# Attention stage of a decoder layer: weight columns laid out for contiguous stack reads, one DMA for the aug rows, a semaphore for each row part

## The chip, the cores and the metric

The kernel runs on one core of one Trainium2 chip. The metric is the device time of one execution in microseconds. Three runs of the kernel before took 932.71, 935.84 and 937.98 us; the median is 935.84.

## The reference

The program is one post-norm decoder layer on x (4 batches of 512 tokens, 256 features) with a context of the same shape:

```
x = layernorm(x + attn(x))                 # one head of 256, causal softmax
x = layernorm(x + xattn(q=x, k=ctx, v=ctx))
x = layernorm(x + ffn(x))                  # 8 experts, the best 2 for each token, and a shared expert

def xattn(q, k, v):                        # 16 heads of 16 features, blocks of 128 tokens
    Q, K, V = (heads(t @ W.T + b) for ...)
    loc   = softmax(Qb @ Kb.T / 4) @ Vb                      # the query's own block
    cross = softmax(Qb @ K[window of 3 blocks].T / 4) @ V    # own block and its neighbours
    return (loc + cross) @ Wo.T + bo
```

Everything is in float32. The kernel gets that accuracy on TensorE by splitting operands into a high and a low part (float32r) and summing high x high, high x low and low x high.

## The kernel before

**Stages.** The attention stage treats the batches one after the other and takes the first 450 us. Then come routing and the shared expert, then 39 tiles of 128 slots for the experts, then the last norm. The change is in the cross attention alone.

**Halves.** The 16 heads of a batch are treated in two halves of 8. `half(a, c)` on PE (L1466) has 16 units. In each it computes, for half `a`, raw scores of two heads (L1507), from which VectorE takes maxima (L1023), and for the half `c` before it the scores again, now with the maxima subtracted (L1522 for the own block, L1528 for the neighbours), which ScalarE exponentiates (L697) and PE multiplies with V (L1473, L1487). So half `a` and half `c` run interleaved, one stage apart. Between two halves PE has other work: the first attention of the next batch (`glue_and_attention1`) or the projections of the next batch (`project2`).

**The stack.** A head has only 16 features. To fill TensorE's rows, the three products of high and low parts are stacked: `k_stack` holds for each pair of heads 32 partitions of high rows, 32 of low and 32 of high again; `q_stack` holds for each head its high, high and low rows, at partitions 32 * section + 16 * parity, the other 16 partitions of a section being zero. So one matmul of 96 rows gives the full product. Rows 96 to 99 of `q_stack` are the aug rows: the negated maxima and their differences, in high and low parts, which meet ones in `k_stack`.

**How a stack is filled.** The projections leave keys and queries with features on partitions. SP writes them to DRAM, high and low separately (`rows_away`, L263, into `k_rows` and `q_rows`), waits for those writes, and reads them back into the stack (`stack`): 3 DMAs of 256 KB for the keys (L275) and 12 of 64 KB for the queries (L283). The feature order is head by head, so the 512 tokens of one feature, 2 KB, are what lies together on the DRAM side when heads of one half are read into one partition. PE waits for the keys and the first six query reads before a half (`stacked`, L1501) and for the other six at its middle (`stacked_late`, L1503). The aug rows go from `augT` (32 partitions) to four partitions of `q_stack` by four DMAs, one for each (`aug_rows`, L290).

**What sets the order.** SP issues all these DMAs, in program order, in one queue; a wait of SP holds up all that is behind it. From one batch to the next the order is: key rows of half 0, aug rows of half 1 of the batch before, query rows of half 0, loop edge, keys and queries of the stack of half 0, key and query rows of half 1, x_raw; later aug rows of half 0, the stack of half 1, c_raw. `keep_clock` is a run of matmuls without use that only occupies PE.

Of the kernel before, what the change touches and what calls it, by code (L numbers as in the profile page):

```python
# [21 lines left out]
F = mybir.dt.float32  # L22
# [3 lines left out]
ALU = mybir.AluOpType  # L26
AX = mybir.AxisListType.X

P = 128
B, S, D = 4, 512, 256  # L30
# [5 lines left out]
HEADS, DH = 16, 16  # L36
HALF = HEADS // 2
# [23 lines left out]
PAIRS = HALF // 2  # L61
# [8 lines left out]
def build(nc, x_d, xT_d, cT_d, w_d, brow_d, bcol_d, gate_w_d, gate_b_d,  # L70
          w1_d, b1T_d, w2_d, b2_d, ws1_d, bs1T_d, ws2_d, bs2_d, out_d):
    ctx = ExitStack()
    with ctx:  # L73
# [3 lines left out]
        def sem(name):  # L77
            return ctx.enter_context(nc.semaphore(name))
# [143 lines left out]
                                            for n in ("xs_in", "yw_sent", "st_step", "st_sent"))  # L222
        k_away, q_away, stacked, stacked_late = ([sem(f"s_{n}{h}") for h in range(2)]
                                                 for n in ("k_away", "q_away", "stacked", "stacked_late"))
# [13 lines left out]
        def _(sp):  # L238
# [20 lines left out]
            def rows_away(b, h, rows, src, away, j):  # L259

                for part, ready in enumerate(("qk2_hi", "qk2_lo")):
                    sp.wait_ge(s[ready], 4 * b + 2 * h + j)
                    sp.dma_start(rows[h, part], src[:, h, part, :].bitcast(F)).then_inc(away[h], 16)  # L263

            def keys_away(b, h):
                rows_away(b, h, k_rows, k_s, k_away, 1)

            def queries_away(b, h):
                rows_away(b, h, q_rows, q_s, q_away, 2)

            def stack(b, h):

                sp.wait_ge(k_away[h], 32 * b + 32)
                for sec, part in ((0, 0), (2, 0), (1, 1)):
                    sp.dma_start(k_stack[32 * sec:32 * sec + 32, h * PAIRS:(h + 1) * PAIRS, :].bitcast(F),  # L275
                                 k_rows[h, part].rearrange("(g p) t -> p g t", g=PAIRS)).then_inc(stacked[h], 16)
                sp.wait_ge(q_away[h], 32 * b + 32)
                for part_done, g0 in ((stacked, 0), (stacked_late, PAIRS // 2)):
                    for par in range(2):
                        for sec, part in enumerate((0, 0, 1)):  # L280
                            r = 32 * sec + 16 * par
                            at = h * HALF + 2 * g0 + par
                            sp.dma_start(q_stack[r:r + 16, at:at + HALF // 2 - 1:2, :].bitcast(F),  # L283
                                         q_rows[h, part].rearrange("(g a p) t -> a p g t", g=PAIRS, a=2)
                                         [par][:, g0:g0 + PAIRS // 2, :]).then_inc(part_done[h], 16)

            def aug_rows(b, h):
                sp.wait_ge(s["augT_out"], 2 * b + h + 1)
                for r in range(4):
                    sp.dma_start(q_stack[96 + r:97 + r, h * HALF:(h + 1) * HALF, :].bitcast(F),  # L290
                                 augT[r * HALF:(r + 1) * HALF, :].bitcast(F)).then_inc(s["aug_in"], 16)

            def body(b, first, last):
# [5 lines left out]
                stack(b, 0)  # L299
                keys_away(b, 1)  # L300
                queries_away(b, 1)
# [13 lines left out]
                stack(b, 1)  # L315
                if not last:
                    sp.wait_ge(s["v_set"], b + 1)
                    sp.dma_start(c_raw[:, :, :], cT_d[:, bass.ts(nb, S)].rearrange("(k p) t -> p k t", p=P))\
                        .then_inc(s["c_raw_in"], 16)
                    keys_away(b + 1, 0)  # L320
                aug_rows(b, 1)
                if not last:
                    queries_away(b + 1, 0)

            keys_away(0, 0)
            queries_away(0, 0)
# [261 lines left out]
        def _(act):  # L588
# [6 lines left out]
            def aug_rows(a, free):  # L595
                if free:
                    act.wait_ge(s["aug_in"], 64 * a)
                act.wait_ge(s["augT_ps"], a + 1)
                copy(augT[:, :], ps[0:4 * HALF, 3, :], "augT_out")
# [55 lines left out]
            def project2(b, c, g):  # L655
# [9 lines left out]
                if c is not None:  # L665
                    for h in range(2):
                        act.wait_ge(k_away[h], 32 * b)
                        act.wait_ge(q_away[h], 32 * b)
# [170 lines left out]
        def _(dve):  # L839
# [175 lines left out]
            def half(a, c, h, ln=None):  # L1015

                if a is not None:
# [12 lines left out]
                    at = 3 * a  # L1030
                    dve.wait_ge(s["a_red"], UNITS * a + UNITS)
# [3 lines left out]
                    nc.vector.tensor_copy(aug[:, :, 0, :], ncross[:, :, :]).then_inc(s["aug_step"], 1)  # L1035
                    dve.wait_ge(s["aug_step"], at + 2)
                    nc.vector.tensor_tensor(aug[:, :, 1, :], ncross[:, :, :], aug[:, :, 0, :].bitcast(F), ALU.subtract)
                    nc.vector.tensor_copy(aug[:, :, 2, :], dloc[:, h, :, :]).then_inc(s["aug_step"], 1)
                    dve.wait_ge(s["aug_step"], at + 3)
                    nc.vector.tensor_tensor(aug[:, :, 3, :], dloc[:, h, :, :], aug[:, :, 2, :].bitcast(F), ALU.subtract)\  # L1040
# [246 lines left out]
        def _(pe):  # L1287
# [178 lines left out]
            def half(b, a, c, ha, hc, full, v2=None):  # L1466
# [26 lines left out]
                if c is not None:  # L1493
                    pe.wait_ge(s["k_ones"], 1)
                    pe.wait_ge(s["aug_in"], 64 * (c + 1))
                for u in range(UNITS):
                    if a is not None:
# [14 lines left out]
                    if c is not None:  # L1512
# [8 lines left out]
                        qv = q_stack[:, 2 * p:2 * p + 2, :]  # L1521
# [254 lines left out]
```

## Time and profile before

| | |
|---|---|
| median of 3 runs | 935.84 us |
| the profiled execution's own time | 933.65 us |
| its span | 931.9 us, mean granted clock 0.907 |
| PE busy | 830.1 us (89%) |
| VectorE, ScalarE, GpSimd busy | 397.5, 346.7, 242.0 us |
| DMA | 76.83 MB, mean 82 GB/s |
| PE at L1507 (raw scores) | 88.9 us, idle before it 16.2 us |

Busy time is the time in which an engine executes; "idle before" is the time for which it stood still ahead of a group of instructions, with what it waited for. PEclk (also "granted clock") is the TensorE clock that the throttle granted, as a share of 2.4 GHz. The profile shows one execution; its 933.65 us is 2.19 below the median of the three timed runs.

### The profile page before, as it was taken

What the parts mean: (1) busy time and instruction counts of PE and PEld (TensorE: products, weight loads), DVE (VectorE), ACT (ScalarE), POOL (GpSimd) and SP (SyncE); (2) the same over time, 40 slices, a digit from 0 to 9 for tenths busy, and PEclk for the clock granted to TensorE, in tenths of its full rate; (3) what the DMA queues carried; (4) which work ended last, traced back from release to release, by engine and by line L of the source; (5) the groups of instructions that cost most, each with busy time, mean ns of one, the idle gap of its engine ahead of it and who ended that gap; (6) DMA issues with size and microseconds to landing.
All of it is one profiled execution on the core that took longest, in us unless ns stands there. A gap on an engine that the chain in (4) does not pass through costs nothing. (4 is left out here: it accounts for less than half of the span.)

```text
span 931.9 us, 15553 instructions
## 1 busy us (share of the span) xinstructions
PE 830.1 (89%) x4992; PEld 626.3 (67%) x4993; DVE 397.5 (43%) x746; ACT 346.7 (37%) x898; POOL 242.0 (26%) x258
## 2 busy tenths in 40 slices
PE   6689988999898989999579998999999999999930
PEld 4567765777567656766479997666777777666620
DVE  4736574568346844452376552211222222222216
ACT  1122454346343633255254430333333333333313
POOL 6912111123111401020416775211111111111106
PEclk9987995799669975999889999999999999999975
DMA  9962133121404080300191115541111101111035
GB/s 305 159 178 51 47 94 91 44 52 50 135 2 91 19 231 3 70 4 2 49 363 42 57 52 131 182 158 34 34 34 34 33 29 34 34 34 32 19 108 179
DMA packets 61045, 76.83 MB, mean 82 GB/s; under 512 B 16112, under 2 KB 41584, under 8 KB 60880
## 3 DMA queue, kind: packets, MB, share of 16 engines
q1 hardware_dynamic: 57600, 66.99, 25.9%
q0 software_dynamic: 3408, 9.34, 2.8%
q8 instruction: 23, 0.38, 0.2%
q14 instruction: 14, 0.11, 0.0%
HBM read 50.82 MB, written 24.98 MB: 81 GB/s over the span
## 5 line engine op out<-in xcount | busy, mean ns | idle before, releaser
L1023 DVE TENSOR_REDUCE mx<-ps 128x4 f32<-128x512 f32 (+1 forms) x128 | 104.4, 821 | 95.4 <-PE ps L1507 93.9
L1694 PE MATMUL ps<-we,hT 128*128 x624 | 142.8, 382 | 2.5 <-ACT hT L795 2.5
L1694 PEld LDWEIGHTS ps<-we,hT 128*128 128x128 f32 x624 | 119.7, 192 | 35.5 <-issue 20.9
L1674 PE MATMUL ps<-we,xT 128*128 x312 | 140.6, 593 | 1.9 <-issue 1.9
L1224 DVE COPY hp<-ps 128x512 f32<-128x512 f32 x78 | 50.2, 686 | 158.5 <-PE ps L1674 158.5
L1507 PE MATMUL ps<-k_stack,q_stack 96*128 96x256 f32 (+1 forms) x256 | 88.9, 441 | 16.2 <-DMA q_stack<-q_rows 14.2
L795 ACT ACTIVATE hT<-ps,b1T 128x128 f32<-128x128 f32 x312 | 84.9, 383 | 35.2 <-PE ps L1685 35.2
L1674 PEld LDWEIGHTS ps<-we,xT 128*128 128x128 f32 x312 | 56.2, 190 | 58.1 <-issue 58.1
L697 ACT ACTIVATE pT<-ps 128x256 f32<-128x256 f32 x128 | 49.2, 385 | 117.9 <-PE ps L1522 113.1
L1507 PEld LDWEIGHTS ps<-k_stack,q_stack 96*128 96x128 f32 x256 | 50.6, 246 | 54.5 <-issue 24.4
L590 ACT ACTIVATE xT<-ps 128x256 f32<-128x256 f32 x39 | 14.9, 384 | 180.9 <-PE ps L1657 180.9
L566 POOL CAST yidx<-meta 128x1 int32 (+1 forms) x39 | 7.2, 184 | 238.6 <-ACT yw L804 238.6
L700 ACT ACTIVATE pT<-ps 128x256 f32<-128x256 f32 (+1 forms) x128 | 62.4, 487 | 0.9
L232 PE MATMUL ps<-xT_s,ws_s 128*128 128x256 f32 x384 | 49.8, 291 | 11.0 <-DVE xT_s L841 9.2
L1232 DVE TENSOR_TENSOR ysum<-ps,b2b 128x256 f32<-128x256 f32 x39 | 16.6, 424 | 95.2 <-PE ps L1694 95.2
L232 PEld LDWEIGHTS ps<-xT_s,ws_s 128*128 128x128 f32 x384 | 48.7, 200 | 11.7 <-issue 11.7
L1528 PE MATMUL ps<-q_stack,k_stack 98*128 98x256 f32 (+1 forms) x128 | 54.3, 424 | 0.0
L1292 PE MATMUL ps<-w_s 128*128 128x512 f32 x218 | 52.2, 393 | 0.0
L232 PE MATMUL ps<-ws_s,h_s 128*128 128x256 f32 x384 | 47.9, 284 | 0.0
L232 PEld LDWEIGHTS ps<-ws_s,h_s 128*128 128x128 f32 x384 | 46.5, 191 | 0.5 <-DVE ws L1144 0.5
L569 POOL DMA_INDIRECT pair_out<-yw,yidx x39 | 38.2, 980 | 29.6 <-POOL yidx L566 29.6
L1292 PEld LDWEIGHTS ps<-w_s 128*128 128x128 f32 x218 | 40.1, 188 | 8.1 <-issue 0.2
(214 smaller groups left out, 1246.1 us busy)
## 6 DMA issues: line engine op xcount, KB each, us to landing
we<-in_w SPq DMA_DIRECT2D x16, 1024.0 KB, 10.6
k_stack<-k_rows SPq DMA_DIRECT2D x24, 256.0 KB, 4.0
q_stack<-q_rows SPq DMA_DIRECT2D x96, 64.0 KB, 4.1
slot_rows<-attn SPq DMA_DIRECT2D x1, 4992.0 KB, 25.0
xs<-slot_rows SPq DMA_DIRECT2D x39, 128.0 KB, 2.1
k_rows<-k_s SPq DMA_DIRECT2D x16, 256.0 KB, 2.3
q_rows<-q_s SPq DMA_DIRECT2D x16, 256.0 KB, 2.8
yl<-pair_out SPq DMA_DIRECT2D x4, 1024.0 KB, 9.5
```

The costliest lines, as they stand in the source:

```text
L232: m = nc.tensor.matmul(out, lhs(a), rhs(b), start=first and n == 0, stop=last and n == 2, skip_group_check=check)
L569: pool.indirect_dma_start(out=pair_out, out_offset=bass.IndirectOffsetOnAxis(ap=yidx[:, q, :], axis=0), in_=yw[:, q, :], in_offset=None).t ...
L697: nc.scalar.activation(pT[:, m % 2, u % 2, 0:2 * P], ps[:, bank, 256:512], ACT.Exp, scale=SCALE2)\
L700: nc.scalar.activation(pT[:, m % 2, u % 2, 2 * P:2 * P + w], ps[:, bank + 1, 0:w], ACT.Exp, scale=SCALE2).then_inc(s["b_exp"], 1)
L795: last = nc.scalar.activation(hT[:, c, :], ps[:, 4 + c // 4, (c % 4) * P:(c % 4 + 1) * P], ACT.Gelu, bias=b1T[:, bass.ds(e * NH + c, 1)])
L1023: nc.vector.tensor_reduce(mx[:, n, 2 * p:2 * p + 2, r0:r0 + nb], ps[:, 2 * (u % 2):2 * (u % 2) + 2, 0:nb * P].rearrange("p h (b k) -> p h ...
L1224: last = nc.vector.tensor_copy(hp[:, c * 512:(c + 1) * 512], ps[:, 2 + c, :])
L1292: nc.tensor.matmul(ps[:, bank, :], w[:, 0:P], w, start=True, stop=True)
L1507: m = nc.tensor.matmul(ps[:, 2 * (u % 2) + j, 0:nb * P], q_stack[0:96, ha * HALF + 2 * p + j, n * P:(n + 1) * P], k_stack[0:96, ha * (HALF ...
L1528: nc.tensor.matmul(ps[:, bank + 1, 0:w].rearrange("p (h n q) -> p h n q", h=2, q=P), k_stack[0:98, p, i * P:(i + 1) * P], qv[0:98, :, :].r ...
L1674: m = nc.tensor.matmul(ps[:, 2 + c, :], xT[:, q, k, :], w[:, bass.ds(e, 1), k * HID + c * 512:k * HID + (c + 1) * 512].rearrange("p o n -> ...
L1694: m = nc.tensor.matmul(ps[:, 6, 0:D], hT[:, c, :], w[:, bass.ds(e, 1), KD * HID + c * D:KD * HID + (c + 1) * D].rearrange("p o n -> p (o n)"),
```

## The change

On the host, the columns of the query and key weights (and the entries of their biases) are put into another order: within a half of 128 features from (pair g, parity a, feature r) to (parity a, feature r, pair g). Row r * 4 + g of `k_rows` then follows row r * 4 + g - 1 of the same partition, so one partition of the key stack reads 4 rows of 2 KB that lie together in DRAM, 8 KB; a query read takes two such rows, 4 KB, for each partition. In `q_stack` the heads of one parity now lie side by side, four and four, and PE's and VectorE's views are adapted.

The twelve query reads are issued in another order: of each group of six, first the high rows (two sections, two parities each), then the low ones; before, it was parity by parity. High and low row DMAs have their own semaphores, so a read waits only for the part that it reads. The four aug DMAs of a half become one, of 64 KB.

```diff
-            def stack(b, h):
-                sp.wait_ge(k_away[h], 32 * b + 32)
-                for sec, part in ((0, 0), (2, 0), (1, 1)):
-                    sp.dma_start(k_stack[32 * sec:32 * sec + 32, h * PAIRS:(h + 1) * PAIRS, :].bitcast(F),
-                                 k_rows[h, part].rearrange("(g p) t -> p g t", g=PAIRS)).then_inc(stacked[h], 16)
-                sp.wait_ge(q_away[h], 32 * b + 32)
+            def stack_keys(b, h):
+                for part, secs in ((0, (0, 2)), (1, (1,))):
+                    sp.wait_ge(k_away[2 * h + part], 16 * b + 16)
+                    for sec in secs:
+                        sp.dma_start(k_stack[32 * sec:32 * sec + 32, h * PAIRS:(h + 1) * PAIRS, :].bitcast(F),
+                                     k_rows[h, part].rearrange("(r g) t -> r g t", g=PAIRS)).then_inc(stacked[h], 16)
+            def stack_queries(b, h):
                 for part_done, g0 in ((stacked, 0), (stacked_late, PAIRS // 2)):
-                    for par in range(2):
-                        for sec, part in enumerate((0, 0, 1)):
-                            r = 32 * sec + 16 * par
-                            at = h * HALF + 2 * g0 + par
-                            sp.dma_start(q_stack[r:r + 16, at:at + HALF // 2 - 1:2, :].bitcast(F),
-                                         q_rows[h, part].rearrange("(g a p) t -> a p g t", g=PAIRS, a=2)
-                                         [par][:, g0:g0 + PAIRS // 2, :]).then_inc(part_done[h], 16)
+                    for part, secs in ((0, (0, 1)), (1, (2,))):
+                        sp.wait_ge(q_away[2 * h + part], 16 * b + 16)
+                        for sec in secs:
+                            for par in range(2):
+                                r, at = 32 * sec + 16 * par, h * HALF + PAIRS * par + g0
+                                sp.dma_start(q_stack[r:r + 16, at:at + PAIRS // 2, :].bitcast(F),
+                                             q_rows[h, part].rearrange("(a r g) t -> a r g t", a=2, g=PAIRS)
+                                             [par][:, g0:g0 + PAIRS // 2, :]).then_inc(part_done[h], 16)

             def aug_rows(b, h):
                 sp.wait_ge(s["augT_out"], 2 * b + h + 1)
-                for r in range(4):
-                    sp.dma_start(q_stack[96 + r:97 + r, h * HALF:(h + 1) * HALF, :].bitcast(F),
-                                 augT[r * HALF:(r + 1) * HALF, :].bitcast(F)).then_inc(s["aug_in"], 16)
+                sp.dma_start(q_stack[96:100, h * HALF:(h + 1) * HALF, :].bitcast(F),
+                             augT[:, :].bitcast(F)).then_inc(s["aug_in"], 16)
...
-                    nc.vector.tensor_copy(aug[:, :, 0, :], ncross[:, :, :]).then_inc(s["aug_step"], 1)
+                    nc.vector.tensor_copy(by_pair(aug[:, :, 0, :]), ncross4).then_inc(s["aug_step"], 1)
...
-                                                 q_stack[0:96, ha * HALF + 2 * p + j, n * P:(n + 1) * P],
+                                                 q_stack[0:96, ha * HALF + PAIRS * j + p, n * P:(n + 1) * P],
...
-                        qv = q_stack[:, 2 * p:2 * p + 2, :]
+                        at = hc * HALF + p % PAIRS
+                        qv = q_stack[:, at:at + PAIRS + 1:PAIRS, :]
...
+    order = np.arange(D).reshape(2, PAIRS, 2, DH).transpose(0, 2, 3, 1).reshape(D)
+    for n in ("L0_xattn_Wq", "L0_xattn_Wk"):
+        lay[n] = lay[n][:, order]
```

## Rows read from the trace of the kernel before

**Rows 1.** The costliest groups: busy, mean ns of one, idle before.
```profile
L1507 PE MATMUL ps<-k_stack,q_stack 96*128 96x256 f32 (+1 forms) x256 | 88.9, 441 | 16.2 <-DMA q_stack<-q_rows 14.2
```
**Rows 2.** PE in order of time: start, duration, instructions, idle before in brackets.
```profile
142.40 0.80 PE L1507 MATMUL ps<-k_stack,q_stack 96*128 96x256 f32 x2 [4.60 <-DMA q_stack<-q_rows]
...
239.75 0.80 PE L1507 MATMUL ps<-k_stack,q_stack 96*128 96x256 f32 x2 [4.55 <-DMA q_stack<-q_rows]
...
337.53 0.47 PE L1507 MATMUL ps<-k_stack,q_stack 96*128 96x256 f32 x2 [4.26 <-DMA q_stack<-q_rows]
```
**Rows 3.** Windows of four halves: length, busy by engine, granted clock, DMA share, GB/s.
```profile
202.20:221.80 19.60, 19.59 (x193) 12.43 (x193) 18.00 (x42) 12.90 (x33) 8.91 (x6) 1.00 0.01 2
142.40:174.40 32.00, 32.00 (x193) 19.91 (x193) 14.89 (x23) 13.63 (x33) 4.25 (x2) 0.50 0.17 53
239.75:271.84 32.09, 32.09 (x192) 19.91 (x192) 14.89 (x23) 13.64 (x33) 4.25 (x2) 0.50 0.16 50
337.53:369.04 31.51, 31.51 (x192) 19.44 (x193) 14.90 (x23) 13.72 (x33) 0.00 (x0) 0.51 0.31 102
```
**Rows 4.** Windows of 2 us inside two of the waits.
```profile
138.00:140.00 2.00, 0.00 (x0) 0.00 (x0) 0.00 (x0) 0.43 (x1) 0.00 (x0) 1.00 1.08 156
140.00:142.00 2.00, 0.00 (x0) 0.00 (x0) 0.00 (x0) 0.00 (x0) 0.00 (x0) 0.53 1.12 170
...
238.00:240.00 2.00, 0.25 (x1) 0.25 (x2) 0.00 (x0) 0.00 (x0) 0.00 (x0) 0.77 0.78 197
```
**Rows 5.** Two shorter gaps of PE, and a window behind each.
```profile
578.85 3.69 PE L1674 MATMUL ps<-we,xT 128*128 x8 [1.92 <-issue]
...
890.67 5.40 PE L1694 MATMUL ps<-we,hT 128*128 x16 [2.48 <-ACT hT L795]
...
578.00:580.00 2.00, 1.15 (x3) 0.68 (x4) 0.00 (x0) 0.00 (x0) 2.00 (x2) 1.00 1.02 407
892.00:894.00 2.00, 2.00 (x6) 1.55 (x6) 0.00 (x0) 0.00 (x0) 0.98 (x1) 0.50 0.18 66
```
**Rows 6.** SP's DMA issues in order of time, batches 1, 2 and 3.
```profile
133.74 1.33 SPq L275 DMA_DIRECT2D k_stack<-k_rows  x3
...
225.96 1.12 SPq L263 DMA_DIRECT2D k_rows<-k_s  x2
227.19 2.71 SPq L290 DMA_DIRECT2D q_stack<-augT  x4
230.01 1.32 SPq L263 DMA_DIRECT2D q_rows<-q_s  x2
232.05 1.27 SPq L275 DMA_DIRECT2D k_stack<-k_rows  x3
233.37 5.55 SPq L283 DMA_DIRECT2D q_stack<-q_rows  x12
...
329.19 1.31 SPq L275 DMA_DIRECT2D k_stack<-k_rows  x3
330.95 5.43 SPq L283 DMA_DIRECT2D q_stack<-q_rows  x12
```
**Rows 7.** VectorE, the low query rows of half 0, batches 1 and 2.
```profile
130.75 0.75 DVE L844 SCALAR_TENSOR_TENSOR q_s<-ps,bcol,q_s 128x512 fp32r<-128x512 f32 x1 [1.79 <-ACT q_s L593]
...
227.71 0.75 DVE L844 SCALAR_TENSOR_TENSOR q_s<-ps,bcol,q_s 128x512 fp32r<-128x512 f32 x1 [1.00 <-ACT q_s L593]
```
**Rows 8.** Time to landing: query reads issued 235.5 to 235.8; row DMAs of 225 to 232.
```profile
q_stack<-q_rows SPq DMA_DIRECT2D x2, 64.0 KB, 3.8
...
DMA to landing us min/median/max: 2.1/2.2/2.6
```
**Rows 9.** Windows: aug DMAs alone; key reads; row DMAs and x_raw.
```profile
228.50:229.50 1.00, 1.00 (x19) 0.63 (x18) 0.63 (x4) 0.18 (x1) 0.00 (x0) 1.00 0.18 33
135.50:138.00 2.50, 2.11 (x16) 1.70 (x14) 1.20 (x2) 0.76 (x2) 0.00 (x0) 1.00 1.05 263
144.00:146.00 2.00, 2.00 (x11) 1.49 (x14) 1.54 (x2) 1.13 (x4) 0.00 (x0) 0.50 1.06 407
```

More of the change, by code:

```diff
@@ L222, in build @@
                                             for n in ("xs_in", "yw_sent", "st_step", "st_sent"))
-        k_away, q_away, stacked, stacked_late = ([sem(f"s_{n}{h}") for h in range(2)]
-                                                 for n in ("k_away", "q_away", "stacked", "stacked_late"))
+        k_away, q_away = ([sem(f"s_{n}_away{h}_{part}") for h in range(2) for part in ("hi", "lo")] for n in "kq")
+        stacked, stacked_late = ([sem(f"s_{n}{h}") for h in range(2)] for n in ("stacked", "stacked_late"))
         yl_in = [sem(f"s_yl_in{b}") for b in range(B)]
@@ new lines, in rows_away @@
+                    sp.dma_start(rows[h, part], src[:, h, part, :].bitcast(F)).then_inc(away[2 * h + part], 16)
+            def stack_keys(b, h):
[4 more added lines that the diff above has]
+                                     k_rows[h, part].rearrange("(r g) t -> r g t", g=PAIRS)).then_inc(stacked[h], 16)
@@ L298, in body @@
                     sp.wait_ge(s["b_ps"], 2 * UNITS * (2 * b - 1))
-                stack(b, 0)
-                keys_away(b, 1)
-                queries_away(b, 1)
+                stack_keys(b, 0)
+                stack_queries(b, 0)
+                rows_away(b, 1, k_rows, k_s, k_away, 1)
+                rows_away(b, 1, q_rows, q_s, q_away, 2)
                 if not last:
@@ L314, in body @@
                     sp.wait_ge(s["b_ps"], 2 * UNITS * (2 * b))
-                stack(b, 1)
+                stack_keys(b, 1)
+                stack_queries(b, 1)
                 if not last:
@@ L319, in body @@
                         .then_inc(s["c_raw_in"], 16)
-                    keys_away(b + 1, 0)
+                    rows_away(b + 1, 0, k_rows, k_s, k_away, 1)
                 aug_rows(b, 1)
                 if not last:
-                    queries_away(b + 1, 0)
-            keys_away(0, 0)
-            queries_away(0, 0)
+                    rows_away(b + 1, 0, q_rows, q_s, q_away, 2)
+            rows_away(0, 0, k_rows, k_s, k_away, 1)
+            rows_away(0, 0, q_rows, q_s, q_away, 2)
             body(0, True, False)
@@ L596, in aug_rows @@
                 if free:
-                    act.wait_ge(s["aug_in"], 64 * a)
+                    act.wait_ge(s["aug_in"], 16 * a)
                 act.wait_ge(s["augT_ps"], a + 1)
@@ L665, in project2 @@
                 if c is not None:
-                    for h in range(2):
-                        act.wait_ge(k_away[h], 32 * b)
-                        act.wait_ge(q_away[h], 32 * b)
+                    for away in k_away + q_away:
+                        act.wait_ge(away, 16 * b)
                 projected(0)
@@ L1030, in half @@
                     at = 3 * a
+                    by_pair = lambda x: x.rearrange("p n (a g) -> p n g a", a=2)
+                    ncross4 = ncross[:, :, :].rearrange("p n (g a) -> p n g a", a=2)
+                    dloc4 = dloc[:, h, :, :].rearrange("p n (g a) -> p n g a", a=2)
                     dve.wait_ge(s["a_red"], UNITS * a + UNITS)
@@ L1494, in half @@
                     pe.wait_ge(s["k_ones"], 1)
[L1495 removed]
+                    pe.wait_ge(s["aug_in"], 16 * (c + 1))
                 for u in range(UNITS):
@@ L1755 @@
         lay[n] = a[n].T if "xattn" in n or n == "L0_attn_Wv" else a[n]
+    order = np.arange(D).reshape(2, PAIRS, 2, DH).transpose(0, 2, 3, 1).reshape(D)
+    for n in ("L0_xattn_Wq", "L0_xattn_Wk"):
+        lay[n] = lay[n][:, order]
+    a["L0_xattn_bq"], a["L0_xattn_bk"] = a["L0_xattn_bq"][order], a["L0_xattn_bk"][order]
     lay["brow"] = np.stack([a["L0_attn_bo"], a["L0_xattn_bv"], a["L0_xattn_bo"]])
```

11 lines of the change are left out of this document (3 added, 8 removed).

## Prediction

> **What bounds the kernel now.** I read the costliest groups first, then who PE waits for, then PE's order of time around those waits, then the windows of the halves (a half is one call of `half`, 16 units) with their granted clock, and last the SP queue in the same stretch.
>
> TensorE is busy 89% of the span, so its idle time and its clock are what can be won. Its only large wait that touches the change is at L1507: 14.2 us, all of it for q_stack [rows 1]. Three of the four waits make nearly the whole of it: 4.60 us before 142.40, 4.55 before 239.75, 4.26 before 337.53 [rows 2]; the fourth, before the very first half, is the rest, 14.2 - 13.4 = 0.8. They stand at the first half of batches 1, 2 and 3, where the kernel turns from the projections of a batch to its scores.
>
> The windows show that the wait is not the whole price. A half that has both scores and exponentials takes 19.6 us at clock 1.00 (2.4 GHz), and 32.0, 32.1 and 31.5 us at 0.50 (1.2 GHz) [rows 3]. So a slow half costs 31.9 - 19.6, about 12.3 us more than a fast one, and all three slow ones stand behind a long wait. What TensorE did before each fall: it had been idle since 137.80 and the clock fell between 140 and 142 (0.53); idle since 235.2, and it fell inside 238 to 240 (0.77); idle since 333.27, working again from 337.53, and fallen almost at once, since the half from there has 0.51 in the mean [rows 3, 4]. It then stays at 0.50 for the whole half, although PE is busy throughout. The waits themselves are 13.4 us, their clock is 3 x 12.3 = 37 us: the second is the prize.
>
> Shorter gaps are met elsewhere: 1.92 us before 578.85 and the clock stays at 1.00; 2.48 us before 890.67 and it is 0.50 from 892 on [rows 5]. So the outcome is open for a gap near 2 us or a little above.
>
> **The chain that ends the wait.** Batch 2 shows it [rows 6]: SP issues the key rows to DRAM (225.96, 1.12), four aug DMAs (227.19, 2.71), the query rows (230.01, 1.32), goes round its loop (0.72 until 232.05), issues three key reads (1.27) and, from 233.37, twelve query reads (5.55, 0.46 each). PE needs the first six. The sixth is issued at 233.37 + 5 x 0.46 = 235.7, lands 3.8 us later [rows 8], 239.5, and PE starts at 239.75.
>
> **The change, part by part.**
>
> One aug DMA for four. It takes 3 x 0.68 = 2.0 us of issue time off SP, ahead of the query rows. In batch 2 the low query rows are ready at 227.71 + 0.75 = 228.46 [rows 7], so the two row DMAs are issued by about 228.9, and after 0.72 for the loop the key reads start at 229.65 instead of 232.05: 2.4 earlier. In batch 1 the low rows are ready only at 131.50 [rows 7]; issue until 131.95 and 0.7 for the loop make 132.7 instead of 133.74: 1.05 earlier. In batch 3, whose key reads start at 329.19 [rows 6], I take the 2.0 of the issues alone. The aug rows of the other halves are used only after the whole attention of the next batch, some 20 us on; nothing waits there, and nothing is gained.
>
> The price of it: the transfer is now one of 64 KB at one moment. The old ones moved 33 GB/s at a DMA share of 0.18, about three engines' worth [rows 9]. 64 KB at 33 GB/s is 2.0 us; if it sits on few queues, the query rows issued 0.7 us later wait behind it there, and so do the key reads. Bounds: 0 (it spreads, or passes) and 2.0 - 0.7 = 1.3. I take 0.7 in batches 2 and 3 and 0.3 in batch 1, where the query rows come later anyway.
> The Trainium skill, "DMA: Bandwidth & Descriptors", section "Why a DMA increments its semaphore by 16 and not by 1", says that a DMA is spread over the largest number up to 16 that divides the slowest dimension of both sides. For 32 source and 4 destination partitions that is 4 engines, against 8 before; by that rule the delay is nearer the upper bound. No row here shows which engines were used.
>
> Own semaphores for high and low rows. The key reads already wait for nothing (the rows left 5 us earlier). The query reads of batch 3 stood 0.4 us (from the end of the key issues, 330.50, to 330.95) for both row DMAs; now the first four wait for the high rows alone. Gain 0.4 there, none in batch 2, where issue runs straight on [rows 6], and none counted in batch 1. The row DMAs land after 2.1 to 2.6 us [rows 8]: issued at 228.0 and 228.5 they are home by 231.1, and the query reads start at 229.65 + 1.27 = 230.9: covered to 0.2 us. This cover is thin, and is gone if the aug transfer delays them; that is in the 0.7 above.
>
> 8 KB runs (4 KB for the queries, whose reads fetch two heads). Instruction counts and bytes stay: 3 x 256 KB and 12 x 64 KB for each stack. Is the run length what limits these reads? The trace has the answer nearby: the row DMAs and x_raw that follow a stack, also in runs of 2 KB but with 128 partitions on their SBUF side, move 407 GB/s; the key reads (32 partitions) dominate a stretch of 263 GB/s, and while only query reads (16 partitions) are under way it is 156, at a DMA share of 1.05 to 1.10 in all of them [rows 4, 9]. The rate goes with the number of partitions written, and the change leaves it. So I put the gain of longer runs near zero.
> The Trainium skill, "SBUF — State Buffer", section "Door 1: The DMA port swizzle", says that 32 partitions reach 8 of 16 ports and 16 partitions only 4, about 218 and 109 GB/s. The trace agrees in the order and lies above both (263, 156), which fits neighbouring DMAs that overlap on other ports. By that rule alone the gain is nil.
> The order of the query reads does change: low and high 16 partitions of a section now alternate, so neighbours overlap more. Bounds for both together: at best the sixth read lands 2.5 us after issue like the row DMAs, 1.3 us sooner than its 3.8; at worst larger packets queue badly and cost 0.4. I take 0.4 gained, near the lower end, since the nearest rows give the run length no weight.
>
> DVE writes aug through a permuted view: four instructions of 128x32 a half, some 0.2 us each; the stride can add perhaps 0.1 each on a path that PE reaches without waiting. Nothing. PE's moving operand takes heads 8 KB apart instead of 2: same shapes, nothing. Weight columns are reordered on the host.
>
> **The sum**, waits left:
> batch 1: 4.60 - 1.05 + 0.3 - 0.4 = 3.45;
> batch 2: 4.55 - 2.4 + 0.7 - 0.4 = 2.45;
> batch 3: 4.26 - 2.0 - 0.4 + 0.7 - 0.4 = 2.2.
> That is 1.15 + 2.1 + 2.1 = 5.35 us, and 0.3 at the kernel's first half (wait of 0.8), where the query reads no longer need the low rows at once. With 5.65 us off, the profiled execution's 933.65 (span 931.9, 1.75 around it) becomes 928.0. Each first half whose clock stays at 1.00 takes 12.3 more off. By the gaps of [rows 5], one of 3.45 us mostly ends in a fall (I give 1 in 10 to keep the clock), one of 2.45 keeps it 3 times in 10 and one of 2.2 4 times in 10; shorter waits, if the transfers gain more than I allow, would keep it nearly always. Mixing the two, one half kept is the likeliest: 928.0 - 12.3 = 915.7. The profiled execution lies 2.2 below the median of the runs shown (935.84); I forecast 916.
>
> What is late next where a wait ends: nothing near it. PE's next waits in a first half are for ACT and DVE, and at 1.00 the second halves run with the same partners in 19.6 us.
>
> **The rivals.**
> (a) All three fall again: only issue time is won, 928. For: the shortest wait I compute is still 2.2. Against: 1.92 was survived. Chance 0.30.
> (b) Two kept, 903, or three, 890 (with waits of about 1 us, a few us lower still): the reads do profit from long runs or from the alternating order by more than a microsecond. For: the sixth lands after 3.8 us, against 2.1 to 2.6 for rows written from 128 partitions [rows 8]. Against: the 407 GB/s at 2 KB runs. Chances 0.18 and 0.08.
> (c) Slower: the aug transfer becomes the bound. It stands in front of the query rows on the engines that it uses. The reads start at 233.37 now; the aug data begin to move near 228.5, and the rows behind them need about 1 us; so from a transfer of 3.9 us on, the query reads start later than before. On a single engine, at the 12 GB/s that 33 GB/s over a share of 0.18 of 16 engines makes, 64 KB take 5.3 us: 1.4 us later in each batch, clocks fall as now, 933.65 + 4 = 938. Chance 0.04.
> (d) The wait is set by bytes, not by issue: what starts earlier only queues longer, and the query reads land when they do now. 932. For: DMA share above 1.0 until after PE resumes. Against: before the key reads begin it is far below. Chance 0.04.
> One half kept, 916: 0.36.
>
> A change of 0.5% (4.7 us) is about what a measurement can tell. Faster has (a), (b) and the likeliest, 0.92; (a) clears the bound by only 3 us, so I move 0.05 of it, 0.04 to no change, which with (d) makes 0.08, and 0.01 to slower, 0.05 with (c): faster 0.87. The likeliest case's own range is 911 to 920; the range over the cases, 887 to 930, takes in (a) and (b), with the end of three kept halves and waits some 4 us shorter in sum.
>
> **What would show it.** SP: one aug DMA of under 0.9 us, the key reads of batch 2 near 229.7 counted from its own key rows (3.7 us after them instead of 6.1). Windows: GB/s of the read stretch still near 260 and then 160; if it rises above 300 the port reading is wrong. PE's waits at L1507 of 3.45, 2.45, 2.2; granted clock of the three first halves, 1.00 with some 19.6 us or 0.50 with 32. I am wrong if the waits shrink below 1.5 us, if a gap near 2 us always or never drops the clock, or if the aug transfer holds up the query rows.

## The result, and the profile of the changed kernel

Before: 936.13 us median of 8 runs (932.71 to 939.26). Changed: 929.93 of 8 (927.61 to 931.51). The ratio is 0.9929, interval 0.9909 to 0.9948: 6.2 us less, where the forecast had 20 less; the time lies at the very end of the range. It is rival (a) that came: the issue time is won and TensorE's clock falls three times as before. The profiled executions differ by 3.0 alone (933.65 and 930.66), since that of before lies 2.5 us under its median; differences between its trace and another can so come out smaller than the medians say. Where in the kernel those 2.5 us lie is not known.

The costliest groups, against [rows 1]: the idle time put down to q_stack went from 14.2 to 10.5 us.
```profile
L1508 PE MATMUL ps<-k_stack,q_stack 96*128 96x256 f32 (+1 forms) x256 | 87.6, 435 | 12.9 <-DMA q_stack<-q_rows 10.5
```
PE in order of time, the four waits that make up this sum, against [rows 2]:
```profile
65.49 0.83 PE L1508 MATMUL ps<-k_stack,q_stack 96*128 96x256 f32 x4 [0.32 <-DMA q_stack<-q_rows]
...
141.06 0.79 PE L1508 MATMUL ps<-k_stack,q_stack 96*128 96x256 f32 x2 [3.03 <-DMA q_stack<-q_rows]
...
237.90 0.50 PE L1508 MATMUL ps<-k_stack,q_stack 96*128 96x256 f32 x2 [3.24 <-DMA q_stack<-q_rows]
...
334.58 0.47 PE L1508 MATMUL ps<-k_stack,q_stack 96*128 96x256 f32 x2 [3.96 <-DMA q_stack<-q_rows]
```
They are 1.57, 1.31 and 0.30 shorter than before, where 1.15, 2.1 and 2.1 were forecast, and 0.5 at the very first half (0.3 forecast). Batch 1 did better, batch 3 gained nearly nothing.

Windows of the three first halves, columns as in [rows 3]. Each is again some 32 us at half clock:
```profile
141.06:173.10 32.04, 32.04 (x192) 19.87 (x192) 14.96 (x23) 13.63 (x33) 4.25 (x2) 0.50 0.15 50
237.90:269.90 32.00, 32.00 (x193) 19.42 (x194) 15.26 (x24) 14.04 (x34) 4.50 (x3) 0.53 0.16 51
334.58:366.00 31.42, 31.42 (x192) 19.27 (x192) 14.96 (x23) 13.71 (x33) 0.00 (x0) 0.51 0.27 97
```
SP's issues of batches 1 (the key rows and key reads), 2 and 3, against [rows 6]:
```profile
128.42 1.12 SPq L263 DMA_DIRECT2D k_rows<-k_s  x2
...
132.43 1.25 SPq L270 DMA_DIRECT2D k_stack<-k_rows  x3
...
225.41 1.12 SPq L263 DMA_DIRECT2D k_rows<-k_s  x2
226.64 0.67 SPq L287 DMA_DIRECT2D q_stack<-augT  x1
227.43 0.84 SPq L263 DMA_DIRECT2D q_rows<-q_s  x2
228.91 2.42 SPq L270 DMA_DIRECT2D k_stack<-k_rows  x3
231.37 5.52 SPq L281 DMA_DIRECT2D q_stack<-q_rows  x12
...
321.37 1.12 SPq L263 DMA_DIRECT2D k_rows<-k_s  x2
322.61 0.67 SPq L287 DMA_DIRECT2D q_stack<-augT  x1
323.39 0.84 SPq L263 DMA_DIRECT2D q_rows<-q_s  x2
324.49 1.27 SPq L270 DMA_DIRECT2D k_stack<-k_rows  x3
326.93 5.40 SPq L281 DMA_DIRECT2D q_stack<-q_rows  x12
```
The aug DMA takes 0.67 instead of 2.71, and the key reads of batch 2 start 3.50 us after its key rows instead of 6.09, as forecast (3.7). Then two things appear that were not there. The three key reads of batch 2 take 2.42 us of SP instead of 1.27. And in batch 3 SP is done with the key reads at 325.76 but starts the query reads at 326.93: 1.17 us of waiting for the high query rows (0.45 before, for both parts).

What was won at the queue can be followed into the wait. From the issue of the first key read until PE starts the half (the starts of the SP and PE rows of each trace):

| kernel | batch 1 | batch 2 | batch 3 |
|---|---|---|---|
| before | 8.66 | 7.70 | 8.34 |
| changed | 8.63 | 8.99 | 10.09 |

The key reads start 1.53, 2.59 and 2.05 us sooner after their key rows than before (where the key rows of batches 1 and 3 are issued at 128.20 and 324.02). In batch 1 all of it reaches PE; in batch 2 1.29 of it is lost behind the issue, in batch 3 1.75, and what is left are the 1.31 and 0.30 above.

Where it is lost shows in the time to landing. Issues of the query rows of batch 2, then of batch 3, then key reads of batch 2; the last column is us from issue to landing:
```profile
q_rows<-q_s SPq DMA_DIRECT2D x2, 256.0 KB, 3.8
...
q_rows<-q_s SPq DMA_DIRECT2D x2, 256.0 KB, 3.5
...
k_stack<-k_rows SPq DMA_DIRECT2D x3, 256.0 KB, 4.2
```
The query rows behind the single aug DMA land after 3.5 to 3.8 us. In the kernel before, the same stretch has 2.5 for the rows (issued from 229.9) and 3.8 for the key reads (from 232):
```profile
q_rows<-q_s SPq DMA_DIRECT2D x2, 256.0 KB, 2.5
...
k_stack<-k_rows SPq DMA_DIRECT2D x3, 256.0 KB, 3.8
```
So the rows behind the single aug DMA land 1.0 to 1.3 us later than before, and the key reads 0.4 later in batch 2 and 1.0 in batch 3 (5.0 for 4.0). How much of this is the aug transfer is what e11 below tries.

The data rate of the reads did not rise. Windows of 2.5 us that begin 1.5 us after the first key read's issue, batch 1, kernel before and then changed, columns as in [rows 3]:
```profile
135.24:137.74 2.50, 2.31 (x18) 1.96 (x16) 1.46 (x3) 0.60 (x1) 0.00 (x0) 1.00 1.01 264
...
133.93:136.43 2.50, 2.33 (x17) 2.01 (x15) 2.43 (x6) 1.01 (x3) 0.00 (x0) 1.00 1.04 269
```
The same windows of batches 2 and 3 have 304 and 272 GB/s before, 251 and 282 changed. The 2.5 us after them, mostly query reads, have 170, 186 and 179 before and 167, 184 and 148 changed.

### The profile page after: what moved, and what is told of

Read it like the earlier page. It is cut to its first block and busy times, and to the rows that moved or that the text cites. A ratio compares the mean times of both kernels' runs of the same rounds, so it can differ in the third digit from the quotient of the medians.

```text
span 928.9 us, 15535 instructions
## 1 busy us (share of the span) xinstructions
PE 829.9 (89%) x4992; PEld 625.5 (67%) x4993; DVE 398.0 (43%) x746; ACT 346.8 (37%) x898; POOL 242.2 (26%) x258
## 5 line engine op out<-in xcount | busy, mean ns | idle before, releaser
L1508 PE MATMUL ps<-k_stack,q_stack 96*128 96x256 f32 (+1 forms) x256 | 87.6, 435 | 12.9 <-DMA q_stack<-q_rows 10.5
```

The costliest lines, as they stand in the source:

```text
L1508: m = nc.tensor.matmul(ps[:, 2 * (u % 2) + j, 0:nb * P], q_stack[0:96, ha * HALF + PAIRS * j + p, n * P:(n + 1) * P], k_stack[0:96, ha * ( ...
```

## The experiments

The theory after the result: what the change does to SP and the DMAs moves each wait by a microsecond or two, but the time hangs on whether the wait is short enough for TensorE to keep its clock; the landing of rows and reads eats half of what the issues gave. Rivals: long runs or own semaphores are what brought the 6 us; the clock falls at the turn from projections to scores for another reason than the wait.

### Taking the change apart

**e1**: the kernel before, with one aug DMA for four.
```
-                for r in range(4):
-                    sp.dma_start(q_stack[96 + r:97 + r, ...], augT[r * HALF:(r + 1) * HALF, :])
+                sp.dma_start(q_stack[96:100, ...], augT[:, :])
```


> The kernel before with one edit: the four aug DMAs of a half become one of 64 KB; its two semaphore counts follow. Theory A (all of the gain is SP's issue time before the query rows, less what the one aug transfer holds the rows up): the three long waits of PE shrink from 4.6, 4.55, 4.3 to about 3.4, 3.3, 3.7 as in the changed kernel, query row DMAs land after 3.5 to 4.1 us instead of 2.5, time about 930.5. Rival B (the reads' layout and own semaphores carry the gain): the waits stay over 4.2 and the time over 934.


Measured: 934.47 (12 runs) against 936.86 (23 runs of before), ratio 0.9995 (0.9961 to 1.0028). The ratio is nearer to 1 than that of the two medians, since three of the runs of before stand at 924.2 to 925.7. The interval holds 1, so this part alone is not told from no change. Its waits are 3.16, 5.10 and 4.75: shorter in batch 1, longer in 2 and 3. There the query reads, which still wait for both row DMAs, met a low half that landed after 4.1 and 3.4 us. That is not the whole reason: in batch 2 SP starts them at 232.30 even so, 1.07 sooner than before, but the sixth of them lands 5.5 us after its issue, for 4.0 before.

**e2**: the layout alone, that is the long runs and the new places in `q_stack` (four aug DMAs, waits and order as before). **e3**: the changed kernel with four aug DMAs. **e4**: the changed kernel with the weight columns in their old order, so that the reads have runs of 2 KB.
```
# e4
-    k_rows[h, part].rearrange("(r g) t -> r g t", g=PAIRS)
+    k_rows[h, part].rearrange("(g r) t -> r g t", g=PAIRS)
-    lay[n] = lay[n][:, order]
```


> The changed kernel with four aug DMAs again, reads in the old order, each group waiting for both row parts: what is left of the change is the layout, 8 KB and 4 KB runs. Theory A: run length does not limit these reads; waits 4.4 to 4.7 us each, time 935 to 937, GB/s of the query reads 150 to 200 as before. Rival B: longer runs speed the reads, each wait is a microsecond shorter and the time 932 or less. Rival C: the longer pieces overlap worse, waits 0.5 us longer, 937 to 938.

> The changed kernel with the four aug DMAs back. Theory A: query row DMAs land after 2.5 us again, but are issued 2 us later; waits of 4.3 to 4.6 us, time 935 to 936. Rival B: the gain of layout and semaphores stays, waits of 3.5 or less, time 931 or less.

> The changed kernel with the weight columns in the old order, so that every run on the DRAM side is 2 KB again (the row of pair, parity, feature); aug DMA, semaphores, issue order and places in the query stack as changed. Theory A: waits of 3.0, 3.2, 4.0 as in the changed kernel within 0.4, time 930. Rival B: waits a microsecond longer, time 933 or more. Rival C (long pieces hurt): waits shorter by 0.5, time 928.


Measured: e2 940.23 (6 runs), ratio 1.0034 (1.0022 to 1.0046), slower than before. e3 936.24 (12 runs), ratio 1.0 (0.9975 to 1.0025). e4 928.2 (6 runs), ratio 0.9887 (0.986 to 0.9914). The group row of e2 has more idle time for q_stack than before, 17.1 against 14.2:
```profile
L1509 PE MATMUL ps<-k_stack,q_stack 96*128 96x256 f32 (+1 forms) x256 | 89.1, 442 | 19.1 <-DMA q_stack<-q_rows 17.1
```
The waits of e2 are 6.05, 5.49 and 4.85, for 4.60, 4.55 and 4.26. The layout, which the change is named for in the first place, brings nothing: alone it costs 3.4 us, and without the long runs the changed kernel is no slower (928.2 against 929.93, from different sets of runs, so the 1.7 us between them is no finding). The waits of e4 are 2.67, 4.32 and 3.32, 10.3 in sum, against 3.03, 3.24 and 3.96, 10.2 in sum, in the changed kernel, and its windows, placed as above, have 256, 265 and 284 GB/s. So the loss of e2 can't be put on long runs as such; no run parts them from the new places in the old order of the reads. e3 has no gain left: without the single aug DMA the rest of the change, long runs included, is worth nothing that can be measured.

**e9**: own semaphores and the alternating order of the query reads (runs of 2 KB, four aug DMAs). The places in `q_stack` are those of the change too, so it is the kernel before but for all three.


> The kernel before with own semaphores for high and low rows and the new order of the query reads alone (2 KB runs, four aug DMAs). From the trials so far: layout with the old order cost 3.5 us, and semaphores and order on top of it took 4 away. If the parts add, this is 3 to 4 us below before, 932.5 to 933.5, waits of about 4.0 each, because the query reads of two neighbouring DMAs go to different partitions. If the new order only repairs what the long runs spoil, it is 936 to 937 and the waits are 4.3 to 4.6.


Measured: 934.54 (6 runs) against 937.63, ratio 0.9963 (0.995 to 0.9977): 3.1 us. The parts do not seem to add: e1 (-2.4, not told from 0) and e9 (-3.1) make 5.5, together (e4) they bring 8.7. The waits say it more plainly: in sum 0.4 us less than before in e1, 0.2 in e9, 3.1 in e4. That an early issue is of use only where the query reads need not wait for the low rows would fit this, but is argued and not shown.

### The aug transfer

Three ways around it. **e8** issues the aug DMA from ScalarE's queue (on short runs, with the filler of e7 below); **e10** issues it behind the query rows; **e11** moves only 32 of its 512 tokens (the other scores get stale aug rows), 4 KB for 64, with the same issue.
```
# e10
                 if not last:
+                    rows_away(b + 1, 0, q_rows, q_s, q_away, 2)
+                aug_rows(b, 1)
# e11
-                sp.dma_start(q_stack[96:100, ..., :], augT[:, :])
+                sp.dma_start(q_stack[96:100, ..., 0:32], augT[:, 0:32])
```


> The trial before with the aug DMA issued from ScalarE's queue, right after ScalarE has written augT, instead of SP's. It takes the last 0.65 us off SP ahead of the query rows and puts the aug transfer in another queue. If the aug transfer holds up the rows because it stands before them in the same queue, row DMAs land after 2.5 us again and the waits shrink by a further 1 us each: 888 to 890. If it is contention for the same place in SBUF, rows still land after 3.5 us and nothing changes: 891.

> The changed kernel with the aug DMA of the half before issued behind the query rows instead of ahead of them. Theory A (the aug transfer holds up the row DMAs that follow it): query rows land after 2.1 to 2.6 us again in batches 2 and 3 (3.5 to 4.1 in the changed kernel), the key reads behind it still suffer; waits of 2.9, 2.7, 3.3 and 928. Rival E (the hold-up moves whole to the reads): waits as in the changed kernel, 930.

> The changed kernel with only 32 of the 512 tokens in the aug DMA (4 KB instead of 64 KB); the maxima of the other tokens are left out of the scores. Same issue time, nearly no transfer. Theory A: query rows land after 2.5 us, key reads of batch 2 take 1.3 us to issue instead of 2.4, query reads start 1.1 us earlier, waits of about 2.5, 2.0, 2.4. At such waits the clock should stay at 1.00 in some first halves: the time spreads between 905 and 928. Rival F (bytes of rows and reads alone set the landing): rows still land after 3.5, 930.


Measured: e8 895.26, against 900.19 for the same kernel with SP's queue; the runs of both split (893.6 to 905.6 and 895.1 to 906.7), so most of the difference is one clock more or less and not the queue. In its trace, batch 2, the low key rows, which SP issues in the same half microsecond in which ScalarE issues the aug DMA, and then the query rows behind land late just the same:
```profile
k_rows<-k_s SPq DMA_DIRECT2D x1, 256.0 KB, 4.1
...
q_rows<-q_s SPq DMA_DIRECT2D x2, 256.0 KB, 3.6
```
e10: 934.56, ratio 0.9967 (0.9952 to 0.9983), with waits of 4.63, 4.01 and 4.23. In batch 3 the query rows are home after 2.0 us, but the key reads and the first query read behind the aug DMA take 4.9 and 5.7:
```profile
q_rows<-q_s SPq DMA_DIRECT2D x2, 256.0 KB, 2.0
...
k_stack<-k_rows SPq DMA_DIRECT2D x3, 256.0 KB, 4.9
...
q_stack<-q_rows SPq DMA_DIRECT2D x1, 64.0 KB, 5.7
```
e11: 929.86, ratio 0.9903 (0.9877 to 0.9929), the time of the changed kernel (e10 stands 4.7 us above it, on the same chip), although each wait is shorter:
```profile
139.95 0.62 PE L1508 MATMUL ps<-k_stack,q_stack 96*128 96x256 f32 x2 [2.46 <-DMA q_stack<-q_rows]
...
236.51 0.80 PE L1508 MATMUL ps<-k_stack,q_stack 96*128 96x256 f32 x2 [2.76 <-DMA q_stack<-q_rows]
...
332.25 0.47 PE L1508 MATMUL ps<-k_stack,q_stack 96*128 96x256 f32 x2 [2.34 <-DMA q_stack<-q_rows]
```
That is 0.57, 0.48 and 1.62 less than in the changed kernel: the price of the aug transfer's bytes, 2.7 us in sum, one trace against one. From the first key read's issue to PE's start it has 8.07, 8.50 and 8.47 us. So in batch 3 the aug bytes are 1.62 of the 1.75 that were lost behind the issue, and in batch 2 0.49 of the 1.29. The other 0.80 there is open: SP's three key reads take 2.12 us here still and land after 4.2 as in the changed kernel, and the low query rows land after 3.7. The clock nevertheless fell in all three halves, and only one of its six runs, at 922.01, stands lower than the others, by 8 us.

### The clock

**e5** and **e6** put useless matmuls of 128x512 at the end of the projections of batches 1, 2 and 3, 16 in the kernel before and 12 in the changed one; they write a bank whose content nobody reads.
```
                 if g is not None:
                     pe.wait_ge(s["lgT_out"], g + 1)
+                if c is not None:
+                    keep_clock(12)
```


> The kernel before with 16 matmuls without use (keep_clock, 128x512) on PE at the end of the projections of batches 1, 2 and 3, just ahead of the long wait; they compute nothing that is used. They take 16 x 0.24 = 3.8 us of a wait of 4.3 to 4.6. Theory C (the price of the wait is the clock that falls in it): what is left of each wait is 0.5 to 0.9 us, the halves resume at the same time but at granted clock 1.00 and take 19.6 instead of 32 us, three times: 936 - 37 = 899 +- 3. Rival D (the half is slow for another reason, the long wait only stands before it): no change, 936.

> The changed kernel with 12 such matmuls at the same place (2.9 us of waits of 3.0 to 4.0). Theory C: 930 - 37 = 893 +- 3, waits left of 0.1 to 1.2 us, clock 1.00 in all three first halves. Rival D: 930. If a residual wait of about 1 us after the filler still drops the clock in one, 905.


Measured: e5 913.7 (4 runs) against 937.93, ratio 0.9765 (0.9735 to 0.9794); e6 896.1 (895.85 to 896.51), ratio 0.956 (0.9544 to 0.9577). In e5 waits of 0.88, 1.04 and 1.35 us are left behind the useless matmuls, two clocks are kept and the third falls (0.52 over its half), so it stays 15 us above the 899 expected. e6 has the three first halves at full clock; PE's rows around the turn of batch 1, and the three windows:
```profile
137.44 2.91 PE L1293 MATMUL ps<-w_s 128*128 128x512 f32 x12
140.30 0.51 PE L1510 MATMUL ps<-k_stack,q_stack 96*128 96x256 f32 x2
```
```profile
140.55:160.20 19.65, 19.65 (x194) 12.45 (x194) 14.28 (x22) 13.12 (x34) 4.36 (x3) 1.00 0.26 81
224.32:244.00 19.68, 19.68 (x193) 12.53 (x194) 14.06 (x20) 12.90 (x34) 4.26 (x2) 1.00 0.27 83
308.54:328.00 19.46, 19.46 (x192) 12.16 (x192) 13.99 (x20) 12.87 (x33) 0.00 (x0) 1.00 0.46 162
```
2.91 us of work a batch that computes nothing bring the changed kernel 34 us. The three halves are 12.4, 12.3 and 12.0 us shorter than its own, 36.7 in sum, where 12.3 each was forecast; the two traces have the same work in them. The Trainium skill, "TensorE: Matmul & The Clock Gate", section "What's actually happening", has the clock follow how busy TensorE has lately been. The trace agrees: PE's work before the half was all that the edit changed, and the half takes 19.65 us at 1.00 in place of 32.04 at 0.50.

At the end of the third half e6 is 38 us ahead, at the end of the kernel 34. Some 4 us are lost right behind that half, where PE now waits for VectorE's aug rows:
```profile
330.86 0.61 PE L1317 MATMUL ps<-ident,aug 128*32 128x128 f32 x4 [2.85 <-DVE aug L1041]
...
332.00:335.00 3.00, 3.00 (x16) 2.90 (x15) 0.35 (x2) 0.28 (x2) 0.00 (x0) 0.54 0.52 98
336.00:340.00 4.00, 4.00 (x20) 3.26 (x19) 2.09 (x4) 0.00 (x0) 0.00 (x0) 1.00 1.04 185
```
One cast of VectorE into `aug` takes 2.34 us there, beside an instruction of GpSimd; in the changed kernel it takes 0.19 and is over before GpSimd's starts. That the two hold each other up was not tried.

**e7**, **e15**: the same with runs of 2 KB, 12 and 16 useless matmuls. **e12**: runs of 2 KB, the aug DMA behind the query rows, 12 of them.


> The changed kernel with 2 KB runs again (old order of weight columns) and the same 12 matmuls. If longer runs cost what the pair of trials on them says (about 1.7 us in the whole), this is 1 to 2 us below the filled changed kernel: 891 to 892. If the layout only acts through the clock, it is the same within 1 us.

> All that helped together: own semaphores, new order, one aug DMA behind the query rows, 2 KB runs, and 12 matmuls without use ahead of the wait. Waits left under 0.7 us, clock 1.00 in all three first halves, 893 to 896. If the clock still falls in some executions in the last batch, 905 in those.

> The changed kernel with 2 KB runs (weight columns in their old order) and 16 useless matmuls (3.8 us of work) in place of 12. With 12 its idle times were 0.35, 0.57 and 0.78 and its runs split at 895 and 906. Theory A: 3.8 us cover the waits wholly, all three clocks kept in every run, 894 to 897, since what the filler adds beyond the data's arrival (0.6, 0.3, 0.1) is at most 1 us in sum; long runs then are worth nothing here either (896.1 with them and 12). Rival: the third half still falls in some runs, since the idle time is not what decides there: a split at 895 and 907 again.


Measured: e7 906.73, 905.26, 895.11 and 895.09 (in the first, the profiled one, the clock of batch 3 falls behind a wait of 0.78); e15 897.6 (896.59 to 899.47), ratio 0.9592 (0.9573 to 0.9611), its waits wholly covered; e12 929.71 (913.22 to 937.71), a spread of two clocks, with profiled waits of 2.16, 2.39 and 1.98 where under 0.7 was expected: the reads behind the aug DMA land late as in e10 (key reads of batch 2 after 5.1 us). e6, at 896.1, beats both kernels and is the lowest in which every run agrees; e8's median, 895.26, is not told from it, and one of its runs is 905.58.

**e13** and **e14** are e6 with 4 and 8 useless matmuls.


> The changed kernel with 4 useless matmuls (some 1 us of work) at the end of the projections of every batch that goes on to scores. With 12 (2.9 us of work) the residual idle times were below 0.3, 0.67 and 0.93 us, all three clocks kept, 896 us. Theory A (the idle time decides): 1 us of work leaves 2.0, 2.3 and 3.0 us idle; idle times of 2.0 to 2.8 let the clock fall nearly always so far, so 925 to 931 us, with a run now and then 12 lower. Theory B (any work at that place is enough, since it moves what the throttle sees of the engine): all three kept, 893 to 900. Theory C (the idle times of 2 us or a little above are a coin's toss, as the forecast had it): one or two kept, 903 to 918, and runs that differ by 12.

> The same with 8 (1.9 us of work). Theory A: 1.1, 1.3 and 2.0 us idle; between 0.9 (kept) and 2.0 (fallen), so one or two kept: 903 to 918 in the median and a spread of about 12 between runs. Theory B: 893 to 898, as with 12. Theory C: two or three kept, 895 to 908.


Measured: e13 920.24, 923.11, 915.27, 931.77; e14 907.06, 930.12, 917.85, 916.81. The first of each is the profiled run. PE's waits and the windows behind them, batches 1, 2 and 3, of e13:
```profile
140.82 0.51 PE L1510 MATMUL ps<-k_stack,q_stack 96*128 96x256 f32 x2 [1.55 <-DMA q_stack<-q_rows]
...
226.06 0.80 PE L1510 MATMUL ps<-k_stack,q_stack 96*128 96x256 f32 x2 [3.77 <-DMA q_stack<-q_rows]
...
323.18 0.47 PE L1510 MATMUL ps<-k_stack,q_stack 96*128 96x256 f32 x2 [2.56 <-DMA q_stack<-q_rows]
```
```profile
140.82:160.40 19.58, 19.58 (x193) 12.45 (x193) 14.00 (x20) 12.90 (x33) 4.27 (x2) 1.00 0.28 86
226.06:258.00 31.94, 31.94 (x192) 19.87 (x192) 14.97 (x23) 13.64 (x33) 4.25 (x2) 0.50 0.12 41
323.18:355.00 31.82, 31.82 (x194) 19.32 (x195) 15.03 (x24) 13.92 (x34) 0.11 (x1) 0.52 0.28 96
```
and of e14:
```profile
140.53 0.50 PE L1510 MATMUL ps<-k_stack,q_stack 96*128 96x256 f32 x2 [0.74 <-DMA q_stack<-q_rows]
...
224.84 0.51 PE L1510 MATMUL ps<-k_stack,q_stack 96*128 96x256 f32 x2 [1.92 <-DMA q_stack<-q_rows]
...
320.73 0.47 PE L1510 MATMUL ps<-k_stack,q_stack 96*128 96x256 f32 x2 [1.68 <-DMA q_stack<-q_rows]
```
```profile
140.53:160.20 19.67, 19.67 (x193) 12.54 (x194) 14.07 (x21) 12.90 (x34) 4.27 (x2) 1.00 0.27 84
224.84:256.90 32.06, 32.06 (x194) 19.74 (x195) 15.25 (x24) 13.93 (x34) 4.40 (x3) 0.52 0.15 50
320.73:340.40 19.67, 19.51 (x192) 12.15 (x192) 14.13 (x21) 12.97 (x34) 0.05 (x1) 1.00 0.45 156
```
The two kernels, which differ in nothing but the number of useless matmuls, have the clock kept behind 1.55, 0.74 and 1.68 us and lost behind 3.77, 2.56 and 1.92. Work at that place is not enough by itself (e13 has it, and loses two): at this place the length of the idle time orders the outcomes. Over the profiled executions of all kernels here, the wait before the first half of batches 1 to 3 and what the clock did in it:

| wait, us | kept | fell |
|---|---|---|
| over 3.0 | 0 | all: before, changed, e1 to e4, e9, e10, e13 |
| 1.9 to 3.0 | 0 | e4 2.67; e11 2.34, 2.46, 2.76; e12 1.98, 2.16, 2.39; e13 2.56; e14 1.92 |
| 1.0 to 1.9 | e5 1.04; e13 1.55; e14 1.68 | e5 1.35 |
| under 1.0 | 13: e5, e6, e7, e8, e14, e15 | e7 0.78 |

It is no sharp bound: 1.35 and 0.78 fell, both in batch 3, and single unprofiled runs of e11 (922.01), e4 (920.16) and of the kernel before (3 of 23, at 924.2 to 925.7), whose profiled waits are all over 1.9, are 8 to 13 us lower than their fellows. What differs in batch 3 is open.

Nor does the length decide alone. The wait of 2.85 us for VectorE behind the third half stands in the profiled executions of e6, e8, e14 and e15, each time before the same matmuls. In e6, e8 and e15 the clock fell around it; in e14 it did not:
```profile
343.09 0.61 PE L1317 MATMUL ps<-ident,aug 128*32 128x128 f32 x4 [2.85 <-DVE aug L1041]
...
344.00:347.00 3.00, 3.00 (x23) 2.73 (x22) 1.09 (x5) 0.50 (x2) 0.00 (x0) 1.00 0.43 82
```
And the price of a fall is not one figure: behind this wait the clock was back at 1.00 after 3 to 7 us, behind the waits at the first halves after 30 us and more.

## Why the prediction was wrong

Two steps failed. The waits of batches 2 and 3 came out at 3.24 and 3.96 us, where 2.45 and 2.2 were computed; and the chances given to waits of 2.2 to 2.45 were too good, so that one half kept could be made the likeliest case. The first alone turns the forecast into rival (a); e11 makes it likely that the second would have done so too. That the time lies inside the stated range is rival (a)'s doing, not that of the forecast of 916.

- **What bounds the kernel**: right. The wait is small and its clock is the prize: e6 wins 36.7 of the 37 us computed from [rows 3] in the three halves, and 34 in the whole.
- **The gap that keeps the clock**: this step failed. The prediction took from [rows 5], one gap of 1.92 us that kept it and one of 2.48 that did not, that "one of 2.45 keeps it 3 times in 10 and one of 2.2 4 times in 10", and made one half kept the likeliest case. Had the waits come out as computed, the clocks would most likely have fallen still: e11 has 2.46, 2.76 and 2.34 and the changed kernel's time. By those chances about one run in three should have lost all three clocks there (an estimate); five of its six runs, 929.58 to 930.45, did. Nine profiled waits between 1.9 and 3.0 us at this place lost it and none kept it. One row on either side, from another stage, was too little to set a chance by, all the more as one wait of 2.85 us goes either way (e6, e14); the three falls before stood behind 4.3 to 4.6 and said only that the bound lay below.
- **Issue time**: right. 2.0 us of aug issues less, key reads 1.5 earlier in batch 1 (1.05 forecast), 2.6 in batch 2 (2.4), 2.05 in batch 3 (2.0).
- **The aug transfer**: right in kind, too small. 0.3, 0.7 and 0.7 us were taken; e11, which takes the bytes away, gives 0.57, 0.48 and 1.62, 2.7 for 1.7. In batch 3 it compounds: the high rows land after 3.5 us for 2.0 in e10, and SP itself then stands 1.17 us for them. The forecast named that thin cover (0.2 us) but booked its loss inside the 0.7. That the delay does not hang on the queue is shown by e8, and that order only moves it by e10. That it comes from the few partitions written is not shown: e11 takes away bytes and leaves the shape, and no run writes the 64 KB to more partitions.
- **The landing of the query reads**: not foreseen. Without the aug term the forecast's own sum leaves 3.15, 1.75 and 1.5 us; e11 has 2.46, 2.76 and 2.34, so in batches 2 and 3 1.0 and 0.8 us are missing beside the aug bytes. In batch 3 these are the 0.4 for the semaphores and the 0.4 for the layout and order of the reads: SP does start the query reads right behind the key reads in e11 (0.05 us for 0.45 before), but PE does not start sooner for it, 8.47 us after the first key read's issue, before 8.34. In batch 2 the 0.4 did not come either, and the reads land 0.80 later behind their issue (8.50 for 7.70), which is rival (d) in small; which DMA holds the others up was not settled. In batch 1 the wait is 0.7 shorter than that sum.
- **Long runs worth nothing**: right in sum (e4 for the changed kernel: waits of 10.3 and 10.2 us), and the rates stayed where the forecast had them. But the 0.4 a batch counted for layout and order did not come, and the bound of 0.4 on the bad side was too small: the layout in the old order lengthens the three waits by 1.45, 0.94 and 0.59 (e2).
- **Own semaphores and the alternating order**: 0.4 a batch and 0.4 more in batch 3, 1.6 in sum; by the medians 3.1 (e9), by the idle time of its group row 1.0 (13.2 for 14.2), and of the three waits only that of batch 1 is shorter (3.84, 5.06 and 4.31). So the sum of the issue part (5.65 forecast; 6.2 by the medians, 3.7 by the waits) looks better than its terms.
- **Rivals (c) and (d)**: neither came as a whole. (c)'s mechanism is there, but with query rows that land 1.0 to 1.3 us later, and not with a transfer of the 3.9 us that it needed.
- **The last sum**: 915.7 is on the scale of the profiled execution, which the forecast itself puts 2.2 us below the median, so its figure for the median should have been 918 and not 916. And by its own three chances (1, 3 and 4 in 10) no half kept has 0.38 against 0.46 for one: the likeliest case was hardly likelier than the one that came.

## What to carry to other kernels

Where TensorE idles for a few microseconds and then runs for 30 us at 0.50, ask first for the whole wait, not for a part of it: cutting three waits from 4.5 us to 3.4 gave 6 us here, to 2.5 (e11) no more, and covering them gave another 34, and useless matmuls on a free PSUM bank do the covering. A chance for a clock event is not to be read from one neighbouring gap; and several DMAs merged into one save their issues, but the one then moves its bytes all at once and can be in the way, and what was won at the queue has to be set against the landing of everything near it.

## What the runs showed that was not expected

- Runs of 8 KB instead of 2 KB in DRAM, written to 32 partitions, are not faster: 269, 251 and 282 GB/s against 264, 304 and 272 in windows placed alike, and 256, 265 and 284 with the short runs of e4.
- A DMA of 64 KB into 4 partitions delays a neighbour issued beside it on another queue: the low key rows of e8 land after 4.0 to 4.1 us, the high ones just ahead of them after 2.1.
- In no trace here did a first half whose clock had fallen win it back before its last 0.3 us, though PE was busy throughout, even behind a wait of as little as 0.78 us (e7, batch 3: 0.54 over 32 us).
- The clock can fall after PE has taken up its work again: with PE busy from 308.88 in e7 it is 1.00 until 311 and 0.50 from 312.
- The granted clock can split the runs of one and the same program by steps of 11 to 12 us (e7: 895.1 and 906.7; e14: 907.1, 917.9, 930.1), so that the median of few runs says little there.
